# Reordering three places of a fused LoRA and memory FFN kernel: the seam of its two phases, a fold in each batch, and the queues of the last stores

## The reference

```
h      = x @ W.T + bias + (x @ A[ids].T) @ B[ids].T          # per-batch LoRA of rank 16
query  = h @ Wq.T ; scores = (query @ Wr.T) @ (keys @ Wr.T).T / sqrt(48) + log_rel
top 8 of 512 slots -> attn = query . keys / 8 + log_rel -> softmax over the 8
aux    = (softmax @ values) @ Wvd.T @ Wvu.T
learned = gelu(h @ Wu1.T + bu1) @ Wu2.T + bu2
u      = clip(0.5 * log1p(var h) / mean(log1p(var h)) + 2.5 * sigmoid(learned), 0, 5)
gate   = sigmoid(gate_w1 * clip((u - 0.5) / 1.5, 0, 1) + gate_bias), 0 below 0.05
out    = x + h + gate * aux
```

## Time and profile before

| | us |
|---|---|
| median of three runs | 1915.87 (1915.84 to 1920.31) |
| the profiled execution | 1916.47 |
| its span in the trace | 1913.9 |
| TensorE busy | 1898.0 (99%) |
| VectorE busy | 1286.4 (67%) |
| ScalarE busy | 714.2 (37%) |
| GpSimd busy | 397.4 (21%) |

### The profile page before, as it was taken

The page is one execution under the profiler, slowest core; times in us unless marked ns, Lnnn a source line. Parts: engine busy times, 40 slices in busy tenths (PEclk is TensorE's granted clock), DMA queues, the critical chain, the costliest instruction groups (busy, mean ns, idle before and its releaser), DMA issues.

```text
span 1913.9 us, 24642 instructions
## 1 busy us (share of the span) xinstructions
PE 1898.0 (99%) x8480; PEld 1550.8 (81%) x8480; DVE 1286.4 (67%) x1686; ACT 714.2 (37%) x1133; POOL 397.4 (21%) x275
## 2 busy tenths in 40 slices
PE   8999999999999999999999999999999999999998
PEld 6888888888888888888888888877888888888887
DVE  5786788565468746447864745777776677677676
ACT  4332344333234333224433333445444234333333
POOL 2210232020023202002310100220443323322332
PEclk9999999999999999999999999999999999999999
DMA  7856877451456745146664425666988777777797
GB/s 279 305 180 216 288 250 230 153 181 60 149 201 232 241 144 179 55 157 216 230 219 146 165 91 192 233 202 226 319 276 286 232 239 243 233 237 247 228 363 295
DMA packets 195633, 412.35 MB, mean 215 GB/s; under 512 B 26740, under 2 KB 28276, under 8 KB 195382
## 3 DMA queue, kind: packets, MB, share of 16 engines
q1 hardware_dynamic: 150006, 321.64, 51.2%
q10 hardware_dynamic: 45504, 89.15, 12.2%
HBM read 313.17 MB, written 97.52 MB: 215 GB/s over the span
## 4 chain that ended last, share of the span: by engine, by line
PE 95%; DVE 3%; ACT 1%; issue 1%; DMA 0%; ACTq 0%; DVEq 0%; SPq 0%
PE bank L1915 21%; PE bank L1916 21%; PE bank L1917 21%; PE bank L1954 6%; PE bank L1955 6%; PE bank L1956 6%; PE bank L1858 2%; PE bank L2074 2%; PE bank L1859 2%; PE bank L2076 1%; PE bank L2075 1%; PE bank L1846 1%; PE bank L1972 1%; PE bank L1971 1%; PE bank L2039 1%
## 5 line engine op out<-in xcount | busy, mean ns | idle before, releaser
L1915 PE MATMUL bank<-xop,wsp 128*128 128x512 f32 x1792 | 701.8, 392 | 6.0 <-DVE wsp L1342 6.0
L1916 PE MATMUL bank<-xop,wsp 128*128 128x512 f32 x1792 | 700.3, 391 | 0.0
L1917 PE MATMUL bank<-xop,wsp 128*128 128x512 f32 x1792 | 699.2, 390 | 0.0
L1915 PEld LDWEIGHTS bank<-xop,wsp 128*128 128x128 f32 x1792 | 337.4, 188 | 85.4 <-DVE wsp L1342 6.4
L1917 PEld LDWEIGHTS bank<-xop,wsp 128*128 128x128 f32 x1792 | 337.1, 188 | 71.8
L1916 PEld LDWEIGHTS bank<-xop,wsp 128*128 128x128 f32 x1792 | 337.6, 188 | 70.6
L909 ACT ACTIVATE wsp<-wraw 128x1024 fp32r<-128x1024 f32 x184 | 195.0, 1060 | 495.7 <-PE bank L1917 487.8
L1342 DVE TENSOR_TENSOR wsp<-wraw,wsp 128x1024 fp32r<-128x1024 f32 x184 | 234.8, 1276 | 154.9 <-ACT wsp L909 154.1
L891 POOL TENSOR_TENSOR r_h<-r_h,r_x 128x512 f32<-128x512 f32 x128 | 175.3, 1370 | 358.3 <-DMA r_h<-h_dram 322.9
L1954 PE MATMUL bank<-h_sp,wu 128*128 128x512 f32 x512 | 200.5, 392 | 1.4 <-DVE stage L1428 1.4
L1955 PE MATMUL bank<-h_sp,wu 128*128 128x512 f32 x512 | 199.8, 390 | 0.0
(11 more groups left out here) (187 smaller groups left out, 1953.7 us busy)
## 6 DMA issues: line engine op xcount, KB each, us to landing
xraw<-in_x SPq DMA_DIRECT2D x248, 256.0 KB, 4.2
wraw<-in_w SPq DMA_DIRECT2D x123, 512.0 KB, 3.8
wraw<-t_dram SPq DMA_DIRECT2D x80, 512.0 KB, 3.6
h_dram<-stage ACTq DMA_DIRECT2D x128, 256.0 KB, 2.7
hraw<-h_dram SPq DMA_DIRECT2D x128, 256.0 KB, 4.1
r_x<-in_x SPq DMA_DIRECT2D x128, 256.0 KB, 4.4
r_h<-h_dram SPq DMA_DIRECT2D x128, 256.0 KB, 3.6
out<-o_st ACTq DMA_DIRECT2D x96, 256.0 KB, 3.9
```

The source lines that it names most:

```text
L1915: pe.matmul(ps, wsp[:, slot, 0, f], x_hi(i), start=(k == 0), stop=False)
L1916: pe.matmul(ps, wsp[:, slot, 0, f], x_lo(i), start=False, stop=False)
L1917: last = pe.matmul(ps, wsp[:, slot, 1, f], x_hi(i), start=False, stop=(k == HT - 1))
```

## The change

Four edits, all of them in the order of instructions:

1. At the seam: DVE does `finish(TILES - 2)` before the splits of tile `TILES - 1`'s turn and `finish(TILES - 1)` right behind them, ahead of the `add_sums` of an older tile. The last `add_sums` moves behind `h7_lo(0)` in step 0 of phase two, and the split of the last pair of Wu1 blocks (`split_wu_hi(7)`, `split_wu_lo(7)`) moves into step 2.
2. `fold_acc(b)` moves from k = 0 to k = 2, behind `selected` of the first token tile.
3. `learned_pass(b)` moves from the start of step k = 2 into the `u_pass` of k = 3, ahead of group m = 2, and `sigmoid_learned(b)` from k = 2 to k = 3 on ACT, ahead of `exp_tile`.
4. SP stores only the even blocks of the last batch; ACT stores the odd ones at the end of its stream.

```diff
@@ sync
-            for o in range(KT):
+            for o in range(0, KT, 2):
                 store7(o)
@@ scalar, end of phase one
             square_and_store(TILES - 2)
-            split_wu_hi(7)
             square_and_store(TILES - 1)
@@ scalar, steps of phase two
                 if c == 0:
                     h7_hi(k)
+                if step == 2:
+                    split_wu_hi(7)
...
-                    if k == 2:
+                    if k == 3:
                         sigmoid_learned(b)
                     if k in MASK_AT:
                         exp_tile(POS[b, MASK_AT[k]])
@@ scalar, end
             evacuate(5)
             evacuate(6)
+            for o in range(1, KT, 2):
+                act.wait_ge(last7_ready, o + 1)
+                act.dma_start(out[NB - 1, o], r67[o][:, 1, :]).then_inc(last_out, 16)
@@ vector, tiles of phase one
                 if g == LAST + M3 * HT + 1:
                     keys_lo()
+                if g == TILES - 1:
+                    finish(g - 1)
                 if p == NPAIR - 1 and q == M3:
                     if o < 6:
                         split_wu_lo(o)
...
                     if o >= HT - 2:
                         h_lo(o - HT + 2)
+                if g == TILES - 1:
+                    finish(g)
                 if g > 1 and tile_of(g - 2)[1] in H_PRODUCTS:
                     add_sums(g - 2)
-                if g > 0 and tile_of(g - 1)[1] in H_PRODUCTS:
+                if 0 < g < TILES - 1 and tile_of(g - 1)[1] in H_PRODUCTS:
                     finish(g - 1)
-            finish(TILES - 1)
             add_sums(TILES - 2)
-            split_wu_lo(7)
-            add_sums(TILES - 1)
@@ vector, steps of phase two
                 if c == 0:
                     h7_lo(k)
+                    if k == 0:
+                        add_sums(TILES - 1)
+                    if k == 2:
+                        split_wu_lo(7)
                     if k in (2, 4):
                         fold_sums(NB - 2 + (k - 2) // 2)
...
                         query_sum(b)
-                        fold_acc(b)
                     if k == 1:
                         query_lo(b)
...
                     if k in SCORE_AT:
                         selected(POS[b, SCORE_AT[k]])
+                    if k == 2:
+                        fold_acc(b)
@@ tensor
             def u_pass(step):
...
                 for m in range(FT):
+                    if k == 3 and m == 2 and c >= 1:
+                        learned_pass(c - 1)
...
-                    if k == 2:
-                        learned_pass(b)
```

More of the change, by code:

```diff
@@ L1940, in _, with learned_pass @@
             lora_b(TILES - 1)
+            def learned_pass(c):
+                wait(pe, zl_ready, c * (TT // 2))
+                if c < NB - 1:
+                    pe.wait_ge(acc_step, ACC_STEPS * (c + 1))
+                    pe.matmul(folded_ps, same[:], part[:, 0:TT * GROUPS], start=True, stop=True).then_inc(learned_done, 1)
+                    return
+                pe.wait_ge(acc_step, ACC_STEPS * c + FT)
+                for t in range(TT):
+                    last = pe.matmul(learned_ps[:, t:t + 1], acc[:, t * P:(t + 1) * P], ones[:, 0:1],
+                                     start=True, stop=True)
+                last.then_inc(learned_done, 1)
             def u_pass(step):
@@ L1981, in query7_pass @@
                     .then_inc(h7_used, 1)
-            def learned_pass(c):
-                wait(pe, zl_ready, c * (TT // 2))
-                if c < NB - 1:
-                    pe.wait_ge(acc_step, ACC_STEPS * (c + 1))
-                    pe.matmul(folded_ps, same[:], part[:, 0:TT * GROUPS], start=True, stop=True).then_inc(learned_done, 1)
-                    return
-                pe.wait_ge(acc_step, ACC_STEPS * c + FT)
-                for t in range(TT):
-                    last = pe.matmul(learned_ps[:, t:t + 1], acc[:, t * P:(t + 1) * P], ones[:, 0:1],
-                                     start=True, stop=True)
-                last.then_inc(learned_done, 1)
             def score_pass(n):
```

## The result

The changed kernel takes 1924.62 us (median, 1921.73 to 1926.47) against 1916.85 us for the kernel before on the same chip (1915.84 to 1920.31); the ratio is 1.0035 [1.0026, 1.0044]. A second set gave 1924.89 against 1918.19, ratio 1.0031 [1.0019, 1.0043]; in brackets behind a ratio stands its 95% interval. The forecast was 1916.2, in a range of 1912.8 to 1918.3: too low by 8.4 us. The profiled execution took 1923.66 us.

The account below looks back on a forecast made before the run. TensorE, busy 1898.0 of 1913.9 us, was taken to bound the kernel. Seam +1.15, fold -0.7 and stores -0.1 sum to +0.35 us, moving the median from 1915.87 to 1916.2, range 1912.8 to 1918.3.

Parts of the forecast that it names:

- Seam, the stall that goes: At the seam, L1954's wait for finish(TILES - 2) goes: 1.6 us together.
- Seam, what is late next: query7_pass(0) waits for h7_lo(0), ending about 1343.7 with r_h landed at 1342.4; TensorE keeps 1.0 to 1.1 us.
- Seam, the price: Work put behind h7_lo(0) delays the fold_sums reduce to 1353.35: +1.15 us, ends -1.1 and +2.3.
- the GpSimd one: At the seam, GpSimd's third add meets the Wu1 split and holds DVE off; not in the sum, only the upper end.
- The fold: Moving the fold behind the first selection gains 3.05 us, gives back 2.35: net -0.7, ends -3.05 and +1.0.
- The gains at k = 1: Waits at k = 1 go: 1.0 us at c = 1, 0.2 each at c = 3 to 6, 1.25 at c = 7.
- given back at k = 4 of c = 7: Tanh, table load and exp delay add_out in the last batch: 0.85 of the 1.25 us come back.
- At c = 5: At k = 4 an add_out that was already late gets later: 0.35 us given back.
- The stores: Last stores from a second queue issue 0.55 us sooner, but DMA engines are full: -0.1 us, ends -0.55 and +0.2.
- B: Rival: GpSimd's third add falls into the Wu1 split, TensorE loses 2.3 us, fold nets nothing: 1918.1; chance 0.18.
- A: Rival: the gains hold, seam -1.1 and fold -1.9: 1912.8; chance 0.30.
- C: Rival: TensorE stands in learned_pass at k = 3 for the fold, 0.3 us in seven batches: 1918.3; chance 0.05.

Follow-up runs that it names:

- e1: The kernel before, unchanged, measured and traced a second time; 1918.00 us, ratio 1.0003.
- e15: The kernel before with GpSimd's adds of phase two cut to one column of 512; 1914.36 us, ratio 0.9980.
- e14: The changed kernel with GpSimd's adds of phase two cut to one column of 512; 1915.30 us, ratio 0.9985 against the kernel before.
- e3: The kernel before with only the moves of fold_acc, learned_pass and sigmoid_learned; 1920.64 us, ratio 1.0017.
- e9: The changed kernel again, in a second set of executions; 1924.89 us, ratio 1.0031 against the kernel before.
- e13: The changed kernel without its second store queue; 1925.32 us, ratio 1.0034 against the kernel before.
- e16: The changed kernel with the split of the last Wu1 tile put back ahead of phase two; 1921.50 us, ratio 1.0017 against the kernel before.
- e4: The kernel before with only the last batch's stores put on two queues; 1918.65 us, ratio 0.9997.
- e7: The kernel before with fold_acc at the end of k = 1 behind query_lo, learned_pass as before; 1923.34 us, ratio 1.0033.
- e2: The kernel before with only the seam's edits (finish, add_sums, split_wu); 1920.82 us, ratio 1.0017.
- e8: The kernel before with learned_pass and sigmoid_learned moved to k = 3, fold_acc as before; 1923.83 us, ratio 1.0035.
- e5: The kernel before with only the two early finishes; 1917.49 us, ratio 1.0006.
- e18: The kernel before with GpSimd's adds made to wait for VectorE's h_lo, plus the two early finishes; 1919.16 us, ratio 1.0005.

## Why the prediction was wrong, by its steps

- **Seam, the stall that goes.** Right against the first trace: L1978 no longer waits, 1.66 us. Part of it was luck of that execution: in e1 the unchanged kernel lost 0.59 us less there.
- **Seam, what is late next.** The place was right (`query7_pass(0)` for `h7_lo(0)`), the size not. I let TensorE keep 1.0 to 1.1 us; it kept 0.3 (1.66 - 1.37). `r_h` was issued at 1337.5 in the time of before, as taken, but was in flight for 5.6 us and not 4.7; it landed 0.7 us after the 1342.4 that I took, and ScalarE's and VectorE's split follow it in line.
- **Seam, the price.** "I take +1.15, with -1.1 and +2.3 as ends" failed: it is +3.0 in the first trace, above the upper end, and more where the clock fell. The place, the group and the order of events were as written (a wait of L1878 for `part`), but the reduce ended at 1355.0 in the time of before, not at 1353.35. Of these 1.7 us, 0.75 are the late `r_h`: `h7_lo(0)` ended at 1344.45, not 1343.7. The other 0.9 are on the way from there to the end of the reduce, 10.6 us in place of 9.65, and the failing term is the GpSimd one, which I had at nothing in the sum and at one further add in the upper end. I had one row of an operation held off and overlooked the one ahead of it: VectorE lost 1.7 us to adds in this stretch before. There are three adds in the stretch, one behind each `h7_lo`, and with everything bunched behind `h7_lo(0)` each found an operation with two SBUF inputs: 3.3 us. Idle time took up part of the difference. With the adds cut the way is 7.7 us, the reduce is in time, and the seam is +0.5 from e15's trace to e14's.
- **The fold.** "The fold's net is -0.7 us, with ends at -3.05 and +1.0" failed, and is the larger error: +1.5 and +4.9 in the two traces of the whole, +3.75 alone, 2.2 in e3's median. The gains at k = 1 came in the first trace: with the learned pair's 0.23 the steps of c = 3 to 6 are 0.45 early at k = 2, so 0.2 each as forecast, 1.15 of 1.25 in c = 7, and 0.55 of 1.0 in c = 1. Two terms were missing altogether. First, the attention matmuls at k = 2 wait for the selection, which costs 2.55 us in c = 2 to 5 of the first trace and 3.1 in e9: VectorE's work does not move up by the fold's 1.35 us but waits for ScalarE. Second, the transposes and reduces of the fold had been a cover under which one of GpSimd's adds in each batch hurt nobody. I had looked for what waits on the fold, and not for what the fold shields. What I counted as given back at k = 4 of c = 7 (0.85) was 0.75 in the first trace and 1.2 to 1.7 in e3, e9, e13 and e16. At c = 5 I counted 0.35 and the step came 0.6 us shorter: its wait before came from two operations of the gate that adds had held off (L1723 with 1.26 and L1733 with 1.15 us in place of 0.17). In e15, in the old order but with the adds cut, this step is shorter by the same 0.6 us.
- **The stores.** Right: -0.1 was forecast, and no gain or loss is measurable in the medians (e4, e13). The DMA engines were full before and after. The 0.8 us by which the tail was longer in both traces of the whole stay open.
- **Rivals.** B had the mechanism (GpSimd's third add in the Wu1 split, deciding once the reduce ends after 1352.2), and its 2.3 us for the seam are the nearest forecast of the 3.0; it got 0.18, and let the fold net nothing. A fell. C fell in the changed kernel, but is what e7 does: a standstill of 0.4 to 1.6 us in seven batches.
- **Not in the sum at all.** The stretches at half clock, 1.7 us each, and the level of the kernel before, which is 1916.9 to 1918.5 rather than 1915.87. In the first comparison it stood at 1916.85, so 1.0 of the 8.4 us by which the forecast was too low is this.

## What to carry to other kernels

Before moving an instruction, list what lies beside it on the other engines: an operation that isn't held off (here a transpose, a reduce, or `add_out` with its PSUM input, none over 0.71 us in any trace) can be what keeps a neighbour's long add away from those that are. On an engine that waits for another at the next step anyway, an operation ahead of that wait can be free and behind it is not; take the idle time after the move from the chain that ends it, and don't assume that the engine's later work moves up. To price such contention, shorten the suspected operation in both kernels and compare the two differences: here that turned 6.7 us into 0.9.

## What the runs showed of the hardware

- A VectorE operation with two SBUF inputs, issued just behind a GpSimd add of the same size (1.29 us alone), took 1.79 us in place of 0.69, and the add itself up to 2.12 there and 2.15 elsewhere in the same trace. Transposes and reduces of the same size kept their 0.69 to 0.71. Operations with one SBUF input are hit as well: L1736 on 128x4 took 1.05 us in three batches in place of 0.17 (1698.50 in the trace after), and in the kernel before the same operation, L1731, up to 1.31.
- TensorE's granted clock fell to 0.50 for 3.4 us in some executions (6.8 once). All eight such stretches stand at a wait of TensorE of 1.8 to 3.0 us: six began 0.1 to 1.6 us behind its end, e2's second and the one in e8's phase one (110.7 to 114.1) shortly before its end. It did not fall at every such wait (3.0 us in the trace after, 1.8 in e5).
- Executions differ by 5.1 us in phase one alone (-0.83 in e18, +4.23 in e8), with no difference in its code but the last 6 us. With the adds of phase two cut, ten executions of the kernel before lie within 2.8 us, where 28 of it uncut on the same chip lie within 6.9; why isn't shown.
